# Two chunks' transposes and gram matrices in one burst every sixteen steps, in place of one chunk's every eight

## What is computed

```python
p = x[:, ROW, :]
q = x[:, COL, :]                 # ROW, COL: the 780 pairs of 40 fields
inner = p * q
h = jax.nn.relu(jnp.einsum('bpe,he->bph', inner, W1) + b1)
logits = jnp.einsum('bph,oh->bpo', h, W2) + b2
attn = jax.nn.softmax(logits, axis=1)
pooled = jnp.sum(inner * attn, axis=1)
return pooled @ Wl.T + bl
```

## Time and profile before

| | before |
|---|---|
| median of 3 runs | 1143.89 us (1143.42 to 1144.12) |
| the profiled execution's own time | 1142.66 us |
| its span from first to last instruction | 1140.8 us |
| PE busy | 1117.5 us, 98% |
| DVE busy | 1053.8 us, 92% |
| ACT busy | 981.2 us, 86% |
| mean granted TensorE clock | 0.995 of full speed |

### The profile page before, as it was taken

One profiled execution on the slowest core, in us unless ns is written; L12 is line 12 of the kernel. 1 busy time (PEld: TensorE's weight loads), 2 busy tenths in 40 slices (PEclk: granted clock), 3 DMA queues, 4 the chain that ended last, 5 costly groups with the idle time before them and its releaser, 6 DMA issues.

```text
span 1140.8 us, 63299 instructions
## 1 busy us (share of the span) xinstructions
PE 1117.5 (98%) x29001; PEld 550.5 (48%) x29001; DVE 1053.8 (92%) x1691; ACT 981.2 (86%) x1219; POOL 0.7 (0%) x6
## 2 busy tenths in 40 slices
PE   6999999999999999999999999999999999999995
PEld 3445444444444444454544544554444444544442
DVE  7999999998999989999899998999999899998983
ACT  5888888888988888888888888888889888898884
POOL 0000000000000000000000000000000000000000
PEclk9999999999999999999999999999999999999998
DMA  2231211312212221122212113122131221222110
GB/s 58 39 70 26 67 30 35 67 29 63 41 29 63 41 56 35 29 65 39 58 35 68 29 34 70 28 64 41 25 67 36 58 39 29 63 41 57 23 25 23
DMA packets 220376, 51.31 MB, mean 45 GB/s; under 512 B 216016, under 2 KB 216016, under 8 KB 220112
## 3 DMA queue, kind: packets, MB, share of 16 engines
q1 hardware_dynamic: 220112, 47.27, 20.2%
HBM read 34.11 MB, written 13.12 MB: 41 GB/s over the span
## 4 chain that ended last, share of the span: by engine, by line
PE 98%; DVE 1%; SPq 1%; DMA 0%; ACT 0%; issue 0%; ACTq 0%
PE slot L296 60%; PE logit_bank L316 30%; PE slot L277 4%; PE slot L264 4%; DMA x_rows<-in_r_x 0%; PE slot L342 0%; SPq L193 0%; ACT hidden L369 0%; DVE weighted L468 0%; SPq L223 0%; SPq L227 0%; SPq L225 0%; SPq L230 0%; DVE logits L448 0%; DVE row_max L452 0%
## 5 line engine op out<-in xcount | busy, mean ns | idle before, releaser
L369 ACT ACTIVATE hidden<-slot,b_col 128x780 f32<-128x780 f32 x1024 | 874.7, 909 | 118.5 <-PE slot L296 118.5
L431 DVE TENSOR_TENSOR inner<-xt 128x760 f32<-128x760 f32 x1024 | 907.8, 943 | 51.3 <-PE slot L296 50.8
L296 PE MATMUL slot<-inner,w_block 64*32 64x390 f32 x16384 | 781.4, 489 | 0.0
L296 PEld LDWEIGHTS slot<-inner,w_block 64*32 64x32 f32 x16384 | 314.1, 107 | 331.0 <-issue 271.3
L316 PE MATMUL logit_bank<-hidden,w_window 64*32 64x390 f32 x8192 | 442.9, 487 | 0.6 <-ACT hidden L369 0.6
L316 PEld LDWEIGHTS logit_bank<-hidden,w_window 64*32 64x32 f32 x8192 | 155.3, 105 | 183.5 <-ACT hidden L369 85.6
L353 ACT COPY xt<-slot 128x640 f32<-128x640 f32 x64 | 44.3, 692 | 20.4 <-PE slot L264 20.4
L264 PE MATMUL slot<-ident,x_rows 128*128 128x128 f32 x320 | 50.1, 288 | 9.7 <-DMA x_rows<-in_r_x 9.7
L438 DVE TENSOR_TENSOR inner<-xt 128x80 f32<-128x80 f32 x256 | 59.4, 232 | 0.0
L264 PEld LDWEIGHTS slot<-ident,x_rows 128*128 128x128 f32 x320 | 34.6, 143 | 49.5 <-issue 44.1
L277 PE MATMUL slot<-xt,x_scaled 64*40 64x40 f32 x4096 | 52.9, 205 | 0.0
(11 more groups left out here) (28 smaller groups left out, 27.0 us busy)
## 6 DMA issues: line engine op xcount, KB each, us to landing
x_rows<-in_r_x SPq DMA_DIRECT2D x128, 160.0 KB, 3.1
gram<-gram_dram SPq DMA_DIRECT2D x32, 400.0 KB, 3.8
gram_dram<-gram_rows SPq DMA_DIRECT2D x512, 12.5 KB
gram_dram<-gram_rows SPq DMA_DIRECT2D x256, 25.0 KB
w_rows<-in_L_rec_W SPq DMA_DIRECT2D x2, 16.0 KB, 2.3
wl_col<-in_L_rec_Wl SPq DMA_DIRECT2D x2, 0.2 KB, 2.3
b_col<-in_L_rec_b SPq DMA_DIRECT2D x2, 0.2 KB, 2.3
w_window<-in_L_rec_W SPq DMA_DIRECT2D x2, 0.2 KB, 2.3
```

Source lines behind the costliest of these rows:

```text
L296: last = nc.tensor.matmul(banks[to:to + QUAD, ab * BANK:ab * BANK + HALF], w1_block[rows, of:of + QUAD], inner[rows, at:at + HALF], start= ...
L369: nc.scalar.activation(hidden[s % RING][:, half * PAIRS:(half + 1) * PAIRS].rearrange("p (a n) -> p a n", a=2), banks_of("layer", s, half) ...
L431: nc.vector.tensor_tensor(window_view(inner, to + half * HALF, [[PAIRS, STEP_DUOS], [SPAN, SHIFTS], [1, SPAN]]), window_view(fields, at + ...
```

## The change

T and G are done for two chunks at once (`GROUP = 2`). After L(s) and S(s-1) with s = 4, 20, 36, ... (s = 16g+4) PE has T(2g+2), T(2g+3), G(2g), G(2g+1) in a row, and ACT, after the relus of the same step, its four copies in the same order. `xt` gets a fourth buffer and `x_scaled` a second. DVE extends and scales the even chunk after the products of step 16g-3 and the odd one after those of step 16g+1. SP loads two chunks in a row and stores two grams in a row. How much is computed does not change.

```diff
     INNER_RING = 8
-    XT_RING = 3
+    XT_RING = 4
+    GROUP = 2
     SLOTS = 3
...
         inner = sb("inner", [P, INNER_RING * STEP])
-        x_scaled = sb("x_scaled", [P, CHUNK_DUOS * FIELDS])
+        x_scaled = [sb(f"x_scaled{s}", [P, CHUNK_DUOS * FIELDS]) for s in range(GROUP)]
         gram_rows = [sb(f"gram_rows{s}", [P, 2, GRAM_PAIRS, FIELDS]) for s in range(2)]
...
-        TURN_AT = -13
-        GRAM_AT = -5
-        SPREAD_AT = -3
-        gram_after = {max(n * CHUNK_STEPS + GRAM_AT, 1 + n): n for n in range(CHUNKS)}
-        turn_after = {n * CHUNK_STEPS + TURN_AT: n for n in range(2, CHUNKS)}
-        spread_after = {max(n * CHUNK_STEPS + SPREAD_AT, 1 + n): n for n in range(1, CHUNKS)}
+        GROUP_STEPS = GROUP * CHUNK_STEPS
+        TURN_AT = -12
+        GRAM_AT = TURN_AT + GROUP_STEPS
+        SPREAD_AT = [-3, 1]
+        def chunks_of(group):
+            return range(group * GROUP, (group + 1) * GROUP)
+        gram_after = {g * GROUP_STEPS + GRAM_AT: g for g in range(CHUNKS // GROUP)}
+        turn_after = {g * GROUP_STEPS + TURN_AT: g for g in range(1, CHUNKS // GROUP)}
+        spread_after = {n // GROUP * GROUP_STEPS + SPREAD_AT[n % GROUP]: n for n in range(1, CHUNKS)}
...
             if s in turn_after:
-                place["turn", turn_after[s]] = len(place)
+                for n in chunks_of(turn_after[s]):
+                    place["turn", n] = len(place)
             if s in gram_after:
-                place["gram", gram_after[s]] = len(place)
+                for n in chunks_of(gram_after[s]):
+                    place["gram", n] = len(place)
...
                     offsets_loaded, 16)
-            for n in range(CHUNKS):
-                if n + 2 < CHUNKS:
-                    sp.wait_ge(slots_filled, count_to("turn", n))
-                    load_chunk(n + 2)
-                store_gram(n)
-                if n % CHUNKS_PER_ROUND == CHUNKS_PER_ROUND - 1:
-                    load_gram(n // CHUNKS_PER_ROUND)
+            for group in range(CHUNKS // GROUP):
+                for n in chunks_of(group):
+                    if n + 2 < CHUNKS:
+                        sp.wait_ge(slots_filled, count_to("turn", n))
+                        load_chunk(n + 2)
+                for n in chunks_of(group):
+                    store_gram(n)
+                    if n % CHUNKS_PER_ROUND == CHUNKS_PER_ROUND - 1:
+                        load_gram(n // CHUNKS_PER_ROUND)
...
                                 banks_of("gram", n)[j * TILE:j * TILE + FIELDS, at:at + FIELDS],
-                                x_scaled[rows, duo * FIELDS:(duo + 1) * FIELDS],
+                                x_scaled[n % GROUP][rows, duo * FIELDS:(duo + 1) * FIELDS],
                                 xt[n % XT_RING][rows, duo * EXT:duo * EXT + FIELDS], start=True, stop=True,
...
                 if s in turn_after:
-                    turn_chunk(turn_after[s])
+                    for n in chunks_of(turn_after[s]):
+                        turn_chunk(n)
                 if s in gram_after:
-                    gram_matrix(gram_after[s])
+                    for n in chunks_of(gram_after[s]):
+                        gram_matrix(n)
             score(STEPS - 1)
...
                 if s in turn_after:
-                    copy_turned(turn_after[s])
+                    for n in chunks_of(turn_after[s]):
+                        copy_turned(n)
                 if s in gram_after:
-                    copy_gram(gram_after[s])
+                    for n in chunks_of(gram_after[s]):
+                        copy_gram(n)
                 for j in range(STEP_DUOS):
...
                     dve.wait_ge(wl_loaded, 2 * 16)
-                else:
-                    dve.wait_ge(slots_filled, count_to("gram", n - 1))
+                if n >= GROUP:
+                    dve.wait_ge(slots_filled, count_to("gram", n - GROUP))
                 whole = xt[n % XT_RING][:, :].rearrange("p (d f) -> p d f", f=EXT)
-                nc.vector.tensor_scalar(x_scaled[:, :].rearrange("p (d f) -> p d f", f=FIELDS), whole[:, :, 0:FIELDS],
+                nc.vector.tensor_scalar(x_scaled[n % GROUP][:, :].rearrange("p (d f) -> p d f", f=FIELDS), whole[:, :, 0:FIELDS],
                                         wl_col[:, 0:1], None, ALU.mult).then_inc(scaled_ready, 1)
```

## The result

The changed kernel takes 1157.76 us (1157.13 to 1158.46, four runs) against 1143.95 us before (1143.42 to 1144.12, four runs): a ratio of 1.012 with a 95% interval of 1.0108 to 1.0133. It is slower by 13.8 us, where 1133.5 was predicted and at most 1139.7. The profiled execution took 1157.25 us, 14.6 more than that of before.

The account below looks back on a forecast made before the run. PE, busy 98% of 1140.8 us, was taken as the bound, so time is the sum of its own work. -11.2 (quads) - 0.3 (double G) + 1.1 (start) = -10.4 us: 1133.5 us from the median, range 1131.8 to 1139.7.

Parts of the forecast that it names:

- The sum: Whole kernel: 11.2 us saved by quads, 0.3 by the double G, 1.1 lost at the start; -10.4 us in all.
- The quad: PE's bursts: a quad costs 2.86 us against 3.22 for two pairs, saving 31 x 0.36 = 11.2 us.
- the lower of the two bounds: New junctions T behind T and G behind G: nothing from below, 6.2 us in all from above; nothing was taken.
- The rival with a junction for each group: PE's junctions belong to each group, not the shape change: half gives 1139.7 us, all 1144.7; chance 0.08.
- Slots and ACT: Four places in a row in a quad: three slots are enough, every margin 0.46 us or more, cost nothing.
- The rival of too few slots: Copies free slots 1.05 us later, PE waits 0.6 us in each quad: 18.6 us, 1152.1 us, slower; chance 0.02.
- The exponentials: ACT in every second quad, 15 times: 0 taken, up to 0.2 us a round, 3 us, allowed for the range.
- The start: L(2) waits for DVE's products, held by ACT's copy of chunk 1, and starts at about 17.8: 1.1 us lost.
- the loss is not repeated: After the start DVE needs 3.6 us for two steps against PE's 3.94, so it causes no further loss.
- SP and x: Stores and loads of x take at most 25 us after a quad, needed after 34: hidden, cost nothing.
- The clock: Rival: the clock falls to its lower level in each quad, 31 x 2.5 = 78 us, 1211 us; chance 0.02.

Follow-up runs that it names:

- e2: The changed kernel with every second gram matmul left out, so two grams are 128 instructions: 1122.49 us, ratio 0.9808 to the kernel before.
- e7: The changed kernel with each quad behind step 16g+3, +4 or +5, first gram 42 to 138 instructions behind a block border; extensions moved: 1133.90 us.
- e8: The changed kernel with each quad behind step 16g+3, +4 or +5, first gram 162 to 256 behind a border (first quad kept); extensions moved: 1170.46 us.
- e3: The changed kernel without the grams' stores and loads after the first round: 1157.54 us, ratio 1.0115 to the kernel before.
- e4: The changed kernel with only the two grams merged, transposes alone behind 16g+2 and 16g+10, odd extension behind 16g+3: 1169.75 us.
- e1: The changed kernel with its very first gram computed twice, moving all later PE instructions by 128: 1159.14 us, ratio 1.0129 to the kernel before.
- e5: The changed kernel with T, T, G behind step 16g+4, the second G alone behind 16g+9, odd extension behind 16g+3: 1139.47 us.
- e6: The changed kernel with the four pieces in the order G, T, T, G, odd extension behind 16g+3: 1140.20 us, ratio 0.9966 to the kernel before.

## Why the prediction was wrong

**The sum lacked a term.** The step that failed is the reading that "nothing holds PE up. So the time is the sum of PE's own work", and with it the quad's cost built from starts in the timeline alone. That was true of before, and it was carried over to a stream of another density. The sum asked of each group for its slot, its data, its clock and its neighbours, and not for its instructions. With 14.6 us measured between the profiled executions (+13.8 between the medians) the account is: -10.4 predicted, -1.2 because a clean quad is 0.04 cheaper than forecast, +0.9 for the exponentials, +22.4 for stalls and what follows them at the quads, +3.4 for late copies of the scores: +15.1, 0.5 more than measured.

**What stood.**
- *The quad.* Clean, S to S is 4.81 (4.83 predicted), T to G 1.24 (1.32), G to L 1.41 (1.40). T behind T and G behind G have no junction, the lower of the two bounds. T to G came out 0.08 lower than forecast because 0.124 for a transpose was a mean: by the starts of the single matmuls the first distance is 0.165 and every other one 0.109, before and after, so five more transposes add 0.55 and not 0.62. The step from the fifth to the sixth, across the two chunks, is 0.109 in all 31 quads, like the rest. By the Trainium skill (TensorEngine Tiling (Array Packing), Key Properties) the drain belongs to a change of tiling mode. The trace agrees: no more than 0.109 from T to T across chunks, 0.20 from the last T to the first G, where the tiles change. The rival with a junction for each group falls, in both forms.
- *Slots and ACT.* In the quad at 198.39 the four copies end at 201.86, and the first relu behind them waits for PE. The margin was real but narrow, as e2 shows: with grams half as long ACT does hold PE. The rival of too few slots named the right sign by the wrong mechanism.
- *The exponentials.* 0.06 us in each of the 15 quads beside them, 0.9 in all, where 0 was taken and 3 allowed.
- *The start.* L(2) starts at 17.77, predicted 17.8, when DVE's products are done (17.72), behind DVE's wait for ACT's copy. The hit is in part luck. S(0) starts at 16.92 in this run and not at 16.01, so PE could not have started L(2) before 17.57, and only 0.2 us are DVE's. S(0) varies from run to run: e7 and e8 start with the same instructions and have it at 16.86 and 16.06. And "the loss is not repeated" fails: DVE works without a pause from 14 us to the first copy of scores at 85 us, which costs 0.4 more than before. The wait:

```profile
13.34 0.33 DVE L423 COPY xt<-xt 128x320 f32<-128x320 f32 x1 [2.16 <-ACT xt L365]
```

- *SP and x.* PE's waits for x are those of the start.

**The clock** did not fall in a quad: stretches with stalled and clean quads are at 1.00 above. It fell once, *behind* a stall of 1.94 us, where the steps' S and L took 3.35 us instead of 1.97:

```profile
661.00:665.00 4.00, 4.00 (x72) 1.73 (x62) 2.80 (x6) 2.97 (x8) 0.00 (x0) 0.57 0.33 49
```

0.57 is the mean of this stretch; from 661.30 to 664.50 it is 0.50, the lower of the two levels, 1.2 GHz of 2.4. PE had been idle for 2 us just before. It cost 1.4 us, counted among the stalls. In e3 the same quad's stall (1.85 us) was followed by the same fall; behind the 2.02 us of the quad shown of e8 the clock stayed at 1.00. Of the Trainium skill's statement that transposes do not count as busy in the same way (TensorE: Matmul & The Clock Gate, Part 4) these runs show no effect: 1.24 us of transposes in every quad left the granted clock at 1.00.

**The late copies of scores** were not in the sum either. The one at step 32 is DVE's late start (above). The other eight follow a state of PE that the kernel before never has. Ordinarily the records of L and S stand one behind the other. Behind some borders they begin to interleave: the last tiles of L start among the first of S, the sixteen starts of a score spread over some 0.5 us or more instead of 0.4, and so it goes on for up to 28 steps, while a step still takes 1.97 us. It ends at the next T, or at the next copy of scores, and there it is paid for. In e7, at the quad after step 51:

```profile
123.81 0.58 PE L329 MATMUL logit_bank<-hidden,w_window 64*32 64x390 f32 x6
123.93 0.49 PE L309 MATMUL slot<-inner,w_block 64*32 64x390 f32 x2
124.14 0.94 PE L329 MATMUL logit_bank<-hidden,w_window 64*32 64x390 f32 x10
125.01 1.31 PE L277 MATMUL slot<-ident,x_rows 128*128 128x128 f32 x10
```

S to T is 1.20 us here instead of 0.79. The ten traces have 150 copies of scores. In the 50 places where the score just before was interleaved (its starts spread over more than 0.48 us), they cost 0.22 to 0.58; the other 100 cost 0.12 to 0.14, except three at step 32, all in kernels with DVE's late start. It is not the distance from the last burst (now behind step 20, before behind step 27) by itself: six copies of the kernel after and eleven of e7 cost 0.12 with their quads where the others have them. A T between ends the interleaving, as behind step 26 in e4. In the kernel after 3.2 of the 22.4 us at the quads are longer ways from S to T, at seven quads. The interleaving itself begins at borders: in e7 all twelve begin 12 to 46 instructions behind one that PE crossed 1.24 to 1.52 us behind the end of the packet, so just when the block came. This is read from the traces, and no run tests it by itself; why the order of tiles then stays shifted is not shown.

**What stays open.** Both edges of the clean positions can be read as borders 3.1 us apart. At 136 the second block has 136 instructions of grams (0.7 us) and 120 of steps (2.4 us), 3.1 us together. At position 41 the first block lasts 3.09 us in the trace and nothing stalls, at 28 2.97 with a loss of 0.15. What is open is why the fetch takes longer in some places, as at positions 34 and 36 in e1. e7 still has losses of 0.1 to 0.5 us at nine clean positions; in seven of them S to T is 0.92 to 1.30, the interleaving again.

## What to carry to other kernels

Merging bursts saves the junctions, but it also makes instructions denser, and a term for that belongs in the sum: count an engine's instructions, and find the shortest time in which 256 of them in a row run. Here 3.1 us and more cost little or nothing, 1.3 cost up to 2 us, and just under 3 it varied. Even a block that comes just in time can cost something later, by the interleaving. If PE idles on "issue" with everything ready, number the instructions at the stalls; if they agree modulo 256, either put slower instructions between the dense ones (e5, e6) or move the dense part within its block (e7), which can decide between faster and slower without a change in the work.

## What the runs showed of the hardware that was not expected

- TensorE's program comes over a DMA queue in packets of 16 KB, 256 instructions: 229 packets with 58,662 instructions, 213 with 4096 fewer. A packet took 0.9 to 1.6 us and started about 0.5 us after PE crossed a border; PE never crossed the next one sooner than 1.20 us behind its end, in ten traces. From border to border a held-up PE took mostly 3.0 to 3.7 us, and no less when the grams' traffic was taken away.
- 256 instructions of 64x40 loads and matmuls run in 1.3 us, so tiny matmuls can outrun the supply by more than a factor of two; a stall was up to 2 us.
- Behind some borders L and S went on interleaved, at an unchanged 1.97 us a step, until a T or a copy of scores, where it cost 0.1 to 0.5 us.
- A first transpose is 0.165 us ahead of the second and each later one 0.109 ahead of the next, also across two chunks.
- A wait for instructions can carry another engine's name in the profile (the 1.72 us "ACT gram_rows" above, with ACT's copy done 1 us before).
- Two kernels that do the same work in almost the same order, e7 and e8, can differ by 3.2% by position within blocks. An edit that only adds instructions ahead of a dense part moves its stalls to other places, as e1 did.
- Behind a stall of 1.9 us the granted clock fell to 0.50 in after and in e3, at the same quad; behind one of 2.02 us in e8 and others of 1.7 us it stayed at 1.00.
